# Expert tiles fetched two steps ahead into four buffers and turned between the products of a step, and GpSimd's norms put in front of its scatter in the last turns

## What is computed

```python
x = _layernorm(x + _L0_attn_ref(x, ...))      # RWKV time mixing and channel mixing
# _L0_ffn_ref:
logits = jnp.einsum('bsd,de->bse', x, router_w) + router_b
top1 = jnp.argmax(jax.nn.softmax(logits, axis=-1), axis=-1)
for i in range(E):                            # E = 8
    h = jnp.einsum('bsd,df->bsf', x, w1[i]) + b1[i]      # 128 -> 1024
    a, g = jnp.split(h, 2, axis=-1)
    y = jnp.einsum('bsh,hd->bsd', a * jax.nn.sigmoid(g), w2[i]) + b2[i]   # 512 -> 128
    out = out + jnp.where((top1 == i)[..., None], y, 0.0)
x = _layernorm(x + out)
x = _layernorm(x + _L1_attn_ref(x, ...))      # linear attention
x = _layernorm(x + _L1_ffn_ref(x, ...))       # soft mixture of experts
```

## Time and profile before

| | |
|---|---|
| median of 3 executions | 739.71 us (737.86 to 739.84) |
| the profiled execution, its own time | 742.24 us |
| its span, first to last instruction | 740.5 us |
| PE busy | 655.2 us, 88% |
| PEld busy | 524.0 us, 71% |
| DVE busy | 465.5 us, 63% |
| ACT busy | 368.6 us, 50% |
| POOL busy | 271.7 us, 37% |
| mean granted TensorE clock | 0.95 of full speed |

### The profile page before, as it was taken

The page is one execution under the profiler, slowest core; times in us unless marked ns, Lnnn a source line. Parts: engine busy times, 40 slices in busy tenths (PEclk is TensorE's granted clock), DMA queues, the critical chain, the costliest instruction groups (busy, mean ns, idle before and its releaser), DMA issues. The chain is left out here.

```text
span 740.5 us, 14606 instructions
## 1 busy us (share of the span) xinstructions
PE 655.2 (88%) x4043; PEld 524.0 (71%) x4044; DVE 465.5 (63%) x1390; ACT 368.6 (50%) x818; POOL 271.7 (37%) x574
## 2 busy tenths in 40 slices
PE   4499899999672798989978899999999999999995
PEld 3487788988561798888934577777776777777773
DVE  4888889887624243444425577776777776777632
ACT  4388777888531343444401445545554544445542
POOL 2323766586454111111134324444333433333200
PEclk9699999999785799999999999999999999999999
DMA  4071111111014565666400000000000000000000
GB/s 139 28 230 43 58 58 43 64 64 40 33 43 133 172 216 174 209 213 200 133 21 8 7 8 15 15 14 14 14 14 14 7 11 11 14 15 8 8 8 14
DMA packets 39457, 46.98 MB, mean 63 GB/s; under 512 B 5184, under 2 KB 31104, under 8 KB 39424
## 3 DMA queue, kind: packets, MB, share of 16 engines
q1 hardware_dynamic: 35520, 39.50, 17.1%
q0 software_dynamic: 3328, 6.82, 3.0%
q10 hardware_dynamic: 576, 0.26, 0.1%
HBM read 34.58 MB, written 7.80 MB: 57 GB/s over the span
## 5 line engine op out<-in xcount | busy, mean ns | idle before, releaser
L436 PE MATMUL banks<-xg_cols,w 128*128 128x128 f32 x624 | 79.5, 283 | 0.0
L463 ACT ACTIVATE gate<-banks,b_cols 128x128 f32<-128x128 f32 x156 | 44.5, 367 | 68.9 <-PE banks L436 68.9
L493 DVE SCALAR_TENSOR_TENSOR hidden<-banks,b_cols,gate 128x128 f32<-128x128 f32 x156 | 44.0, 345 | 55.3 <-ACT gate L463 52.4
L436 PEld LDWEIGHTS banks<-xg_cols,w 128*128 128x128 f32 x624 | 76.4, 200 | 0.0
L1368 PE MATMUL banks<-ffn_w,act_cols 128*128 128x128 f32 x512 | 66.2, 278 | 0.7 <-ACT act_cols L1514 0.7
L1368 PEld LDWEIGHTS banks<-ffn_w,act_cols 128*128 128x128 f32 x512 | 60.8, 192 | 8.4 <-issue 6.8
L1362 PE MATMUL banks<-slots_cols,ffn_w 128*128 128x512 f32 x128 | 64.1, 606 | 0.8 <-ACT slots_cols L1529 0.8
L522 POOL DMA_DIRECT2D xg<-sorted_x x40 | 21.8, 546 | 106.4 <-issue 95.5
L1514 ACT ACTIVATE act_cols<-banks 128x512 f32<-128x512 f32 x64 | 38.2, 597 | 28.2 <-PE banks L1362 28.2
L426 PE MATMUL banks<-w,hidden 128*128 x312 | 42.6, 280 | 8.8 <-issue 8.2
L426 PEld LDWEIGHTS banks<-w,hidden 128*128 128x128 f32 x312 | 38.3, 193 | 11.3 <-issue 11.3
(11 more groups left out here) (240 smaller groups left out, 1630.1 us busy)
## 6 DMA issues: line engine op xcount, KB each, us to landing
w<-w_dram SPq DMA_DIRECT2D x39, 512.0 KB, 3.4
xg<-sorted_x POOLq DMA_DIRECT2D x40, 64.0 KB, 2.9
sorted_y<-y_rows SPq DMA_DIRECT2D x39, 64.0 KB, 2.3
x_in_rows<-x_dram SPq DMA_DIRECT2D x16, 128.0 KB, 2.2
x_res<-x_dram SPq DMA_DIRECT2D x16, 128.0 KB, 2.2
xa<-normed SPq DMA_DIRECT2D x16, 128.0 KB, 2.0
stage<-normed SPq DMA_DIRECT2D x16, 128.0 KB, 2.1
out_dram<-final SPq DMA_DIRECT2D x16, 128.0 KB, 1.8
```

Source lines behind the costliest of these rows:

```text
L436: last = pe.matmul(bank(u, k, c * P, (c + 1) * P), w1[parity][u][:, lo:lo + P], xg_cols[u][:, :], start=True, stop=True)
L463: act.activation(gate[u][:, c, :], bank(u, 2, c * P, (c + 1) * P), ACT.Sigmoid, bias=b1_cols[:, bass.ds(e1 * GC + XC + c, 1)]).then_inc(ga ...
L493: last = dve.scalar_tensor_tensor(hidden[u][:, c, :], bank(u, 1, c * P, (c + 1) * P), b1_cols[:, bass.ds(e1 * GC + c, 1)], gate[u][:, c, : ...
```

## The change

In stage 2, `xg` has two buffers for each u (by the parity of the turn), and a tile's fetch is issued four turns ahead of its own number instead of when its single buffer comes free: in GpSimd's step s, once TensorE has transposed turn s + 2, turn s + 4 is fetched into the buffer that this frees. TensorE transposes both tiles of turn s + 2 behind F of u = 0, ahead of S and F of u = 1, and waits for the copies of the tiles before. ScalarE copies each tile behind the gates of its own u, after a wait for F (`lin_ready`) since F of the same u reads the buffer. GpSimd reads the first rows' numbers before it waits for the scatters and issues the fetches of turns 0 and 1 together. SP waits for the tiles of turn 0 before it issues the `w1` loads of turn 1.

In stage 1, step "CR", GpSimd's `scatter` of turn 6 moves behind the third norms of turn 7 and the two slot operations.

```diff
-        xg = bufs("xg", [P, D])
+        xg = [bufs(f"xg_{parity}", [P, D]) for parity in range(2)]
...
-        tables_ready = sem("tables_ready", expert_sems)
-        vec_moved = sem("vec_moved", expert_sems)
-        b1_turned = sem("b1_turned", expert_sems)
-        b1_cols_ready = sem("b1_cols_ready", expert_sems)
+        tables_ready = sem("tables_ready", rwkv_sems)
+        vec_moved = sem("vec_moved", rwkv_sems)
+        b1_turned = sem("b1_turned", rwkv_sems)
+        b1_cols_ready = sem("b1_cols_ready", rwkv_sems)
...
-        xg_loaded = pair("xg_loaded", expert_sems)
+        xg_loaded = [pair(f"xg_{parity}_loaded", expert_sems) for parity in range(2)]
...   experts_sync
             for turn in range(2):
+                if turn:
+                    for u in range(U):
+                        sp.wait_ge(xg_loaded[0][u], 16)
                 for u in range(U):
                     load_w1(turn, turn, u)
...   experts_tensor, at the end of the body over u
                             last.then_inc(done[u], 1)
-                for u in range(U):
-                    if "T" in parts:
-                        pe.wait_ge(xg_loaded[u], s * 16 + 48)
-                        pe.transpose(bank(u, 0, 0, P), xg[u][:, :], ident).then_inc(xg_turned[u], 1)
+                    if u == 0 and "T" in parts:
+                        for v in range(U):
+                            pe.wait_ge(xg_loaded[h][v], i * 16 + 32)
+                            if "F" in parts:
+                                pe.wait_ge(xg_cols_ready[v], s + 2)
+                            pe.transpose(bank(v, 0, 0, P), xg[h][v][:, :], ident).then_inc(xg_turned[v], 1)
...
-            for u in range(U):
-                pe.sem_inc(xg_turned[u], 1)
...   experts_scalar
-                for u in range(U):
                     if "T" in parts:
-                        act.wait_ge(xg_turned[u], s + 4)
+                        act.wait_ge(xg_turned[u], s + 3)
+                        if "F" in parts:
+                            act.wait_ge(lin_ready[u], s + 2)
                         act.activation(xg_cols[u][:, :], bank(u, 0, 0, P), ACT.Copy).then_inc(xg_cols_ready[u], 1)
...
         def experts_gpsimd(pool):
-            def step(parts, i, h):
-                s = i * 2 + h
-                if "T" in parts:
-                    for u in range(U):
-                        settle(pool, xg_turned[u], s + 3, pool_passed)
-                        row = pool.value_load(tile_rows[0:1, bass.ds((s + 2) * U + u, 1)],
-                                              min_val=0, max_val=SORTED_ROWS - P)
-                        pool.dma_start(xg[u][:, :], sorted_x[bass.ds(row, P), :]).then_inc(xg_loaded[u], 16)
+            def row_of(turn, u):
+                return pool.value_load(tile_rows[0:1, bass.ds(turn * U + u, 1)], min_val=0, max_val=SORTED_ROWS - P)
+
+            def fetch(row, parity, u):
+                pool.dma_start(xg[parity][u][:, :], sorted_x[bass.ds(row, P), :]).then_inc(xg_loaded[parity][u], 16)
+
+            def step(s, h):
+                for u in range(U):
+                    row = row_of(s + 4, u)
+                    settle(pool, xg_turned[u], s + 3, pool_passed)
+                    fetch(row, h, u)
 
             pool.wait_ge(tables_ready, 2)
+            first_rows = [row_of(0, u) for u in range(U)]
             pool.wait_ge(scattered, 16 * TILES)
             pool.wait_ge(zeroed_sem, 16 + 16 * E)
-            expert_pipeline(pool, step)
+            for u in range(U):
+                fetch(first_rows[u], 0, u)
+            for u in range(U):
+                fetch(row_of(1, u), 1, u)
+            for s in (-2, -1):
+                step(s, s % 2)
+            with pool.Fori(0, (STEPS - 4) // 2) as i:
+                step(i * 2, 0)
+                step(i * 2 + 1, 1)
...   GpSimd, stage 1
-                    if "R" in parts and "M" not in parts:
-                        if "C" in parts:
-                            find_places()
-                        scatter()
+                    if parts == "CR":
+                        find_places()
...   behind the slot operations
-                    if "R" in parts and "M" in parts:
-                        find_places()
+                    if "R" in parts:
+                        if "M" in parts:
+                            find_places()
                         scatter()
```

## The result

The changed kernel takes 720.03 us (719.12 to 721.65, 4 runs) where the kernel before takes 739.13 (737.86 to 739.84, 4 runs) on the same chip: a ratio of 0.975, 95% interval 0.972 to 0.977. The profiled execution has a span of 720.0 us (before 740.5) and an own time of 721.65. The forecast was 722.6 us and a span of 723.2.

The account below looks back on a forecast made before the run. TensorE was taken to bound stage 2, losing 14.9 us mostly to holes behind late fetches. Steps 14.4 plus start 2.9 gave 17.3 us, median 739.7 to 722.4, forecast as 722.6; own range 719.5 to 725.5, widened to 729.

Parts of the forecast that it names:

- The steps: Stage 2's 18 steps: early fetch into four buffers closes the loop-edge holes, gaining 14.4 of 14.9 us; bounds 6.1 to 14.9.
- The allowance of 0.05 us an edge: Loop edges of stage 2: 0.05 us left open at each of nine edges, taking the gain from 14.9 to 14.4.
- GpSimd's order in "CR": Stage 1, scatter of turn 6 behind the norms: delays the scatter of turn 7, cost 0.7 us, bounds 0 and 1.5.
- its last lands at 237.8: Scatter of turn 7: starts at 231.6 instead of 230.9, its last transfer landing at 237.8 instead of 237.0.
- The start: Start of the experts: second tile transposed 3.1 us sooner, 0.2 given back; gain 2.9 us, bounds 3.6 and -1.7.
- Stage 3: The stage after the experts: not touched by anything in the change, so no gain counted.
- The sum: Whole kernel: 14.4 + 2.9 = 17.3 us, span 740.5 to 723.2.
- A: Rival: loop edges stay open even with tiles there, nine holes of 0.98 us, 731 us; chance 0.12.
- B: Rival: the start gives nothing, fetches still taking 4 to 5 us beside two loads, 726 us; chance 0.08.
- C: Rival: another engine, VectorE above all, sets the pace, steps of 5.8 to 6 us, 728 us; chance 0.05.
- D: Rival: slower than before, as TensorE's mid-step wait for the copy of u = 1 holds every step; chance 0.03.
- E: Rival: no effect, fetches still late despite two steps' room, needing landings of over 11 us; chance 0.02.

Follow-up runs that it names:

- Experiment 2: Changed kernel with transposes back at the end of the step and both copies behind both gates, keeping four buffers and early fetch: 720.66 us, 0.979.
- 4: Changed kernel with one buffer for each u, so tiles are fetched one step ahead, transposes still in the middle of the step: 730.5 us, 0.991.
- 8: Changed kernel with TensorE's sequencer reading the expert's number twice more, to no use, ahead of the first S of even steps: 729.38 us, one execution.
- experiment 1: Changed kernel with GpSimd's old order in step CR, the scatter of turn 6 ahead of the norms and slot operations: 720.73 us, 0.978.
- experiment 5: The changed kernel again, unchanged, for a second profile: 721.37 us against 737.39 for the kernel before, 0.979.
- 11: Changed kernel with eight useless ScalarE copies ahead of the copy of the tile of u = 1 in each step: 733.79 us, one execution.
- 12: Changed kernel with four useless ScalarE copies ahead of the copy of the tile of u = 1 in each step: 721.38 us, one execution.
- experiment 6: Changed kernel with the scatter of turn 6 cut in two, u = 0 behind find_places, u = 1 behind the slot operations: 721.73 us, 0.979.
- 3: Changed kernel without SP's wait for the tiles of turn 0 before the `w1` loads of turn 1: 724.95 us, 0.984.
- Experiment 7: The split-scatter kernel of experiment 6, with SP also waiting for all scatters before the first `w1` load: 720.51 us, 0.977.
- experiment 10: The kernel before, unchanged, profiled a third time: 737.44 us, one execution.
- experiment 9: The kernel before, unchanged, for a second profile: 736.83 us, 10 runs.

## Why the prediction was right, and where it was off

**The steps: forecast 14.4 us, measured 14.9.** The reading was that a fetch that lands late holds the sequencer, and that its 1.5 us of branch and number load then lie open; with the tile there they lie under F. Experiment 2 shows that the early fetch alone does it, 4 that without it the moved transposes leave half of the loss, 8 that the cover at an edge is real and 0.5 us wide (0.3 in the prediction). The allowance of 0.05 us an edge was not needed. What the prediction took for a property of the kernel, 115.3 us for 18 steps, was one draw, the longest of three: the other two profiles have 110.6 and 113.1. By the mean of the three the steps give 12.6 us.

**GpSimd's order in "CR": forecast 0.7 us lost, measured 0.3 to 0.9.** The scatter of turn 7 starts at v + 12.5 against 11.8, and experiment 1 gives it back; at the first F that is 0.9 us against one profile of the changed kernel and 0.3 against the other. The step that was off is the one behind it: "its last lands at 237.8". It landed at 239.7, after 4.0 us, and the prediction took 2.2 from the rows of before. What it depends on shows when the profiles are sorted by how far behind the last scatter's start the first `w1` load is issued: 0.9 us and the scatter lands in 2.2 (all three of before, experiments 1, 5, 11, 12); 0.6 to 0.7 us and it takes 2.6 to 2.9 (2, 6, 8); 0.2 us and it takes 3.7 to 4.0 (the first profile of the changed kernel, 3, 4). Experiment 7 moves that load alone against 6, and the landing goes from 2.7 to 2.2. The later scatter had slid into the loads, by a margin that a few tenths decide. And a scatter that lands in time gains little: in the changed kernel's second profile it took the 2.2 us forecast, and then the fetches met the loads and took 3.2 and 3.6 us where 2.6 was forecast. From the start of the last scatter to the landing of the last tile of turn 0 the two profiles have 7.4 and 6.8 us, where 6.3 were forecast; before it was 10.1.

**The start: forecast 2.9 us, measured 2.2.** The fetch landed in 2.1 us and not 2.6, the two transposes cost little, but the scatter's late landing took 1.8 of it back: the first F came 1.7 us sooner instead of 3.1 (245.27 to 243.61). Then the clock gave 0.6 us back: the first F ran at 0.50 until 247.0, and the second at 1.00 from 247.1, 3.5 us behind the first product; before, all of 245.1 to 249.9 is at 0.50. The Trainium skill (TensorE: Matmul & The Clock Gate, Part 1) says that the array starts at the lower level after being idle and rises once it has been kept busy; the trace agrees. The hold-back of `w1` is worth 2.6 us (3), so it carries the whole gain of the start, and without it the first F would come later than before. Reading the rows' numbers early was not tried by itself.

**Stage 3: forecast nothing, measured 3.3 us.** This is the term that the prediction did not have, and it is most of the difference between 17.3 and 20.5. The granted clock dips in this stage, where TensorE has holes in each of these kernels. All fourteen profiles fall in line when they are sorted by where it goes to 0.50, leaving out the last 3 us of the stage: nowhere, or only in the first 4 us, and the stage takes 363.7 to 363.9 us (both profiles of the changed kernel, 1, 2, 3, 8, 12); once, 11 us behind the beginning, 364.2 to 364.3 (4, 7); once, 45 to 46 us behind it, 365.4 to 365.7 (10, 6, 11); at 10 to 11 and again at 45 to 47 us, 365.9 and 367.1 (9 and the first profile of before). So the dips, by their number and place, go with most of the 3.3 us; why the first profile of before lies another 1.2 us above experiment 9 isn't shown. The stretch ahead of the later dip and the dip itself, in experiment 10, and the same work in the changed kernel, where it doesn't come:

```profile
410.32:415.32 5.00, 3.20 (x25) 2.47 (x26) 3.14 (x13) 1.88 (x4) 1.42 (x3) 1.00 0.00 0
415.32:420.32 5.00, 5.00 (x17) 3.72 (x17) 0.69 (x1) 3.30 (x5) 1.38 (x3) 0.66 0.00 0
```

```profile
396.19:401.19 5.00, 3.20 (x24) 2.47 (x25) 3.17 (x13) 1.91 (x4) 1.42 (x3) 1.00 0.00 0
401.19:406.19 5.00, 5.00 (x22) 3.39 (x22) 1.89 (x3) 3.55 (x6) 1.60 (x3) 1.00 0.00 0
```

TensorE is busy for 3.20 of the 5 us in both, and the clock falls behind only one of them. All three profiles of before have the later dip and two of the eleven with the change have it (6, 11), so it doesn't belong to the kernel before alone. About 2 us of the gain lie here in the mean. Whether the change makes the dips rarer, by when stage 3 begins, or they fell out so, stays open: no experiment moved the beginning of stage 3 by itself.

**The sum: forecast 17.3 us of span, measured 20.5 from one profile to the other.** The three profiles of before have a mean span of 736.4 us, the two of the changed kernel 718.9, which is 17.5 us less: 12.6 in the steps, 2.4 up to the first S, 0.1 at the end of the experts and 2.4 in stage 3. That this is so near to 17.3 is partly luck. The steps were taken from the slowest profile of three and came out 1.8 us too high, the start 0.5 too high, and stage 3, put at nothing, made up for both. In medians the gain was 19.1 us on the chip of the result and 16.0 on that of experiment 5.

**The rivals.** A (edges stay open) is out by the trace after. B (the start gives nothing) came true in small part, 0.5 to 0.7 us of the 2.9; in the first profile through the scatter's landing, in the second through the fetches'. C is out, every step is 5.58 us. D was given its price: it needs the copy over 1 us later, and at 1.7 us it costs 0.66 us a step; to make the kernel slower than before it would have to be about 2 us, an estimate from these 0.66 us and the 1.05 covered. E is out: a fetch landed in 5.2 us at most, though the landings grew at the faster pace (median of a fetch from 2.9 to 4.0 us, of a `w1` load from 3.4 to 4.6), without a wait for either.

## What to carry to other kernels

An idle stretch that ends on "issue" is not the sequencer's fault until its rows say so: look at when it passed the last wait. If it stood there until a transfer landed, the transfer is late, and the branch and register work behind the wait only shows because of it; take the wait away with another buffer, a step earlier, and both go. And before moving a GpSimd transfer behind other work, follow who waits for its landing: here the norms came 3.4 us sooner and nobody needed them, while the landing came 6 us later and somebody did. And before a term of the sum is read off one profile, take a second: here three profiles of one program lay 4.8 us apart in the stretch that the change was made for.

## What the runs showed of the hardware that I had not expected

- A 64 KB fetch of GpSimd's landed in 2.0 to 2.1 us with little beside it and in 4.4 to 5.0 us beside four 512 KB loads.
- A scatter of 128 rows (512 bytes each) landed in 2.2 us when a 512 KB load was issued 0.9 us behind its start, and in 3.7 to 4.0 when it was issued 0.2 us behind.
- Time saved at the start need not arrive. In experiment 6 the first F came 1.9 us sooner than in 5 and the first S of step 0 only 0.9, since the clock rose 27.4 us behind v where it had risen at 27.3.
- Three profiles of one program gave 110.6, 113.1 and 115.3 us for the same 18 steps. With the holes closed, all eight profiles gave 100.41.
